# Layers' context attention: rotated keys and first queries computed in the step before

## What is computed

```python
pe_q = rope_freqs(x.shape[1], 32)
pe_k = rope_freqs(ctx.shape[1], 32)
for l in range(4):
    h = rmsnorm(x, sg[l])
    x = attn_block(h, h,   sWq[l], sWk[l], sWv[l], sWo[l], sbo[l], pe_q, pe_q, mask) + x
    h = rmsnorm(x, cg[l])
    x = attn_block(h, ctx, cWq[l], cWk[l], cWv[l], cWo[l], cbo[l], pe_q, pe_k, None) + x
    h = rmsnorm(x, fg[l])
    x = gelu(h @ fW1[l] + fb1[l]) @ fW2[l] + fb2[l] + x

def attn_block(xq, ctx, ...):            # 8 heads of 64
    q = apply_rope(split(xq @ Wq) / 8, pe_q)
    k = apply_rope(split(ctx @ Wk), pe_k)
    a = softmax(where(mask, q @ k.T, -max))
    return (a @ split(ctx @ Wv)) @ Wo + bo
# apply_rope(t): the first 32 of 64 columns become t * cos + rotate_half(t) * sin
```

## Time and profile before

| | us |
|---|---|
| median of 3 runs | 4027.64 (4020.51 to 4027.95) |
| profiled execution | 4024.78 |
| its span, first to last instruction | 4022.6 |
| PE busy | 3721.1 (93%) |
| DVE busy | 2719.0 (68%) |
| ACT busy | 1980.9 (49%) |
| POOL busy | 1015.0 (25%) |
| mean granted PE clock | 0.978 of full speed |

### The profile page before, as it was taken

One profiled execution on the slowest core, in us unless ns is written; L12 is line 12 of the kernel. 1 busy time (PEld: TensorE's weight loads), 2 busy tenths in 40 slices (PEclk: granted clock), 3 DMA queues, 4 the chain that ended last, 5 costly groups with the idle time before them and its releaser, 6 DMA issues.

```text
span 4022.6 us, 70135 instructions
## 1 busy us (share of the span) xinstructions
PE 3721.1 (93%) x22966; PEld 2300.2 (57%) x22966; DVE 2719.0 (68%) x8004; ACT 1980.9 (49%) x5746; POOL 1015.0 (25%) x1109
## 2 busy tenths in 40 slices
PE   6999899999999998999988998999999999989997
PEld 4645446566565664566656444456656556645664
DVE  3787767676777745676456886777777776457663
ACT  1733345555555542576428214456555565317653
POOL 0154433222423301101111562322322232010012
PEclk8999999999999999999989999999999999999998
DMA  2100000001000002010210000000000000100101
GB/s 74 48 18 1 1 24 18 25 1 42 1 18 24 2 26 81 2 70 16 62 57 5 18 1 18 7 18 25 18 25 10 32 1 12 67 30 2 64 16 51
DMA packets 37011, 103.89 MB, mean 26 GB/s; under 512 B 3504, under 2 KB 28592, under 8 KB 33200
## 3 DMA queue, kind: packets, MB, share of 16 engines
q1 hardware_dynamic: 34608, 95.20, 6.6%
q0 software_dynamic: 2048, 4.20, 0.3%
HBM read 90.35 MB, written 9.04 MB: 25 GB/s over the span
## 4 chain that ended last, share of the span: by engine, by line
PE 70%; DVE 15%; ACT 7%; issue 5%; POOL 2%; DMA 0%; DVEq 0%; POOLq 0%; ACTq 0%; SPq 0%
PE ps_O L646 13%; PE ps_P L628 8%; PE ps_S L597 6%; PE ps_OUT L792 4%; PE ps_O L628 4%; PE ps_OUT L597 3%; ACT EX L729 3%; PE ps_P L1374 2%; PE ps_P L1666 2%; PE ps_S L1374 2%; PE ps_P L608 2%; PE ps_P L382 2%; PE ps_T L597 2%; PE ps_O L382 1%; PE ps_OUT L1157 1%
## 5 line engine op out<-in xcount | busy, mean ns | idle before, releaser
L646 PE MATMUL ps_O<-wide,V 128*64 128x256 f32 (+4 forms) x5152 | 595.8, 393 | 1.8 <-ACT wide L674 1.8
L729 ACT ACTIVATE EX<-NB,neg 128x154 f32<-128x154 f32 (+3 forms) x768 | 402.5, 530 | 113.8 <-DVE neg L757 113.8
L692 POOL COPY RX<-recips 128x256 f32<-128x256 f32 (+2 forms) x356 | 156.9, 441 | 1114.0 <-DVE recips L772 1105.4
L597 PE MATMUL ps_S<-KT,QT 64*128 64x154 f32 (+7 forms) x1936 | 373.1, 456 | 60.7 <-POOL QT L1679 25.4
L783 DVE TENSOR_TENSOR QT<-ps_O,RS 128x512 f32<-128x512 f32 x212 | 146.6, 692 | 390.4 <-PE ps_O L646 390.0
L676 DVE COPY wide<-ps_P 128x512 f32<-128x512 f32 (+4 forms) x528 | 340.0, 647 | 73.0 <-PE ps_P L628 69.6
L646 PEld LDWEIGHTS ps_O<-wide,V 128*64 128x64 f32 (+4 forms) x5152 | 266.6, 127 | 194.1 <-issue 110.1
L597 PE MATMUL ps_T<-KT,QT 64*128 64x154 f32 (+5 forms) x968 | 322.6, 436 | 3.5 <-ACT EX L729 3.5
L597 PE MATMUL ps_OUT<-KT,QT 64*128 64x154 f32 (+5 forms) x968 | 325.7, 435 | 0.1
L628 PE MATMUL ps_P<-consts,EX 128*128 128x128 f32 (+1 forms) x1956 | 290.8, 285 | 25.0 <-ACT RS L683 11.7
L729 ACT ACTIVATE QT<-NB,neg 128x512 f32<-128x512 f32 (+2 forms) x512 | 311.8, 618 | 0.0
(11 more groups left out here) (516 smaller groups left out, 8106.4 us busy)
## 6 DMA issues: line engine op xcount, KB each, us to landing
weights<-in_w_dram SPq DMA_DIRECT2D x10, 1664.0 KB, 7.0
weights<-in_w_dram SPq DMA_DIRECT2D x2, 6148.0 KB, 17.2
weights<-in_w5next_dram SPq DMA_DIRECT2D x6, 1664.0 KB, 6.6
weights<-in_w_dram SPq DMA_DIRECT2D x2, 4200.0 KB, 13.7
weights<-in_reltab_dram SPq DMA_DIRECT2D x2, 4096.0 KB, 13.4
weights<-in_w_dram SPq DMA_DIRECT2D x8, 640.0 KB, 3.8
weights<-in_w_dram SPq DMA_DIRECT2D x2, 2050.0 KB, 8.5
weights<-in_w_dram SPq DMA_DIRECT2D x2, 2048.0 KB, 8.1
```

The source lines that it names most:

```text
L597: ins = pe.matmul(S4[k][:, a * N:(a + 1) * N], QT[strip, c, qts[a] * P:(qts[a] + 1) * P], self.keys(c)[strip, 0:N], start=True, stop=True)
L646: ins = pe.matmul(O1[self.slot * j:self.slot * (j + 1), q0 * P:(q0 + self.nq) * P], self.value(c * self.hpc + j, kc), self.probs(rd, j)[:, ...
L692: pool.tensor_copy(RX[:, q0 * P:(q0 + self.nq) * P].rearrange("p (n s) -> p n s", s=self.slot), of.unsqueeze(2).broadcast_to([P, self.nq * ...
L729: ins = act.activation(ex[:, a * N:(a + 1) * N], src, ACT.Exp, bias=neg[:, at:at + 1], scale=-1.0 if self.added else 1.0, accum_out=sums[: ...
```

## The change

The context keys of all four chunks and the queries of chunk 0 are made and rotated in the step before, the host. All keys and the first queries then lie in parts of `picked`, a buffer unused in the layers. Keys are made in two pairs, K0 (chunks 0 and 1) and K1 (chunks 2 and 3), 308 columns wide in one bank each, and Q is the first query product. In the host they are late entries: for lane 1's self attention K0 behind iteration 5, K1 behind 6, Q behind 8; for lane 0's context step K0 behind 1, K1 behind 2, Q behind 4. The context step keeps q1 in its front, and q2 and q3 as late entries. Its scores of round 0 wait for the third add of `ready`, and its PE program waits at the start until Q's bank has been read. In iterations without maxima DVE takes late entries behind the last product with the reciprocals. In POOL's program a context step has only q1's add ahead of the power.

```diff
@@ class Attention @@
             def evacuated(self, eng, r, s):
                 e, n = self.seq[s]
+                if e in self.ahead_done:
+                    eng.wait_ge(*self.ahead_done[e])
+                    return
...
+                for j in self.late.get(self.rounds, ()):
+                    late(pool, j)
...
             def dve(self, dve, r, free=None, beside=None, late=None):
                 for i in range(self.steps):
-                    for j in self.late.get(i - 1, ()):
-                        if j != "X":
-                            late(dve, j)
+                    if i < self.rounds:
+                        self.late_dve(dve, i, late)
...
+                    if i >= self.rounds:
+                        self.late_dve(dve, i, late)
                     if beside:
                         beside(i)
@@ class L1Attention @@
-                self.order = [(m, c) for c in range(4) for m in "kq"]
+                self.order = [("q", c) for c in range(1, 4)] if cross else [(m, c) for c in range(4) for m in "kq"]
+                late = {0: [1], 1: [2], 2: ["X"]} if cross else {1: [4], 2: [5, "X"], 3: [6], 4: [7]}
+                n = L.n
+                self.hosts = n == (0 if cross else 1)
+                if self.hosts:
+                    late = ({0: [1], 1: [2, "K0"], 2: ["X", "K1"], 4: ["Q"]} if cross else
+                            {1: [4], 2: [5, "X"], 3: [6], 4: [7], 5: ["K0"], 6: ["K1"], 8: ["Q"]})
...
+            def ahead_pe(self, pe, j, bank):
+
+                r = self.r
+                self.weights(pe)
+                if j == "Q":
+                    pe.wait_ge(r.xT, 1)
+                    pe.matmul(bank[:, :], self.w("wq")[:, 0:P], self.L.XT[:, :], start=True, stop=True).then_inc(r.part, 1)
+                    return
+                for i in range(2):
+                    c = 2 * int(j[1]) + i
+                    ins = pe.matmul(bank[:, i * CTX:(i + 1) * CTX], self.w("wk")[:, c * P:(c + 1) * P], self.L.CT[:, :],
+                                    start=True, stop=True)
+                ins.then_inc(r.part, 1)
...
+                dve.stream_shuffle(part, bank[:, 0:308], HALVES).then_inc(r.part_used, 1)
+                dve.tensor_tensor(two(to), two(bank[:, 0:308]), every2(K("cos")), ALU.mult).then_inc(r.part_used, 1)
+                dve.wait_ge(r.part_used, 2 * n + 1)
+                dve.tensor_tensor(two(part), two(part), every2(K("sin")), ALU.mult).then_inc(r.gate, 1)
+
+            def ahead_pool(self, pool, j):
...
+                pool.wait_ge(r.part_used, 2 * n + 2)
+                pool.wait_ge(r.gate, n + 1)
+                pool.tensor_tensor(to, to, part, ALU.add).then_inc(r.ready, 1)
...
             def pe(self, pe):
                 r = self.r
                 self.weights(pe)
                 pe.wait_ge(r.xT, 1)
+                if self.cross:
+                    pe.wait_ge(r.part_used, 6)
                 pe_table(pe, r, self.front)
```

More of the change, by code:

```diff
@@ L566, in value, with query @@
                 return V[0:self.kc, c * w + h * self.slot:c * w + (h + 1) * self.slot]
+            def query(self, c):
+                return self.query0 if c == 0 and self.query0 is not None else QT[:, c, :]
             def out_chunk(self, c):
@@ L1618, in __init__ @@
                 self.NK, self.src = NK, src
-                self.order = [(m, c) for c in range(4) for m in "kq"]
-                self.att = Attention(8, 64, NK, added=None if cross else (lambda h, qt: L.maskb[:, :]),
[L1621 to L1624, removed]
+                self.order = [("q", c) for c in range(1, 4)] if cross else [(m, c) for c in range(4) for m in "kq"]
[5 more added lines that the diff above has]
+                            {1: [4], 2: [5, "X"], 3: [6], 4: [7], 5: ["K0"], 6: ["K1"], 8: ["Q"]})
+                store = picked[:, :, :].rearrange("p t d -> p (t d)")
+                self.turnedK = store[:, 616 * n:616 * n + 616]
+                self.partsK = [store[:, 1232 + 308 * i:1540 + 308 * i] for i in range(2)]
+                self.turnedQ = store[:, 1848:2360]
+                keys = (lambda c: self.turnedK[:, c * CTX:(c + 1) * CTX]) if cross else (lambda c: KT[:, c, :])
+                queries = ((lambda c: (self.r.rotated, c) if c else (self.r.ready, 3)) if cross else
+                           (lambda c: (self.r.rotated, 2 * c + 2)))
+                self.att = Attention(8, 64, NK, added=None if cross else (lambda h, qt: L.maskb[:, :]),
+                                     keys=keys, queries=queries, late=late)
+                if cross:
+                    self.att.query0 = self.turnedQ
+                self.fronts = 1 if cross else 4
+                ropes = [([self.product(j)], P, self.size(j), "D", "rope", self.dest(j), self.turning(j))
+                         for j in range(self.fronts)]
                 values = [([(src[:, c * kc:(c + 1) * kc], w("wv"))], kc, SEQ, "A", "copy",
@@ L1682, in pool @@
                 self.fresh(pool)
-                self.rotate(pool, 0)
-                self.rotate(pool, 1)
+                for j in range(1 if self.cross else 2):
+                    self.rotate(pool, j)
                 self.prev.pool_tail(pool)
@@ L1687, in pool @@
                     self.nxt.pool_head(pool)
-                self.rotate(pool, 2)
-                self.rotate(pool, 3)
+                for j in range(2, self.fronts):
+                    self.rotate(pool, j)
                 if self.prev.tail_parts > 1:
@@ L1700, in pe @@
                 self.att.x_done = self.nxt.r.xT
+                if self.hosts:
+                    nr = self.nxt.r
+                    self.att.ahead_done = {"K0": (nr.part_used, 2), "K1": (nr.part_used, 4), "Q": (nr.part_used, 6)}
                 self.att.pe(pe, r, ready=[(r.evac_act, self.front.a), (r.evac_dve, self.front.d)], wo=self.w("wo"),
```

45 lines of the change are left out of this document (40 added, 5 removed).

## The result

The changed kernel takes **4041.2 us** (median of 6 runs, 4039.56 to 4051.62); the kernel before, on the same chip, 4024.07 (6 runs, 4018.28 to 4038.10). The ratio is 1.0046, 95% interval 1.0032 to 1.0059: slower by 0.46%, where I forecast 4024.6 and a range up to 4037. The profiled executions took 4042.21 and 4024.78. In the experiments, "against" is the kernel before, timed beside the run on the same chip.

A forecast was written before the change was run, and what follows sets the result against it. The head was taken as bound by DVE's time to the first maximum plus an unchanged chain. 1.90 - 0.15 - 2.13 = -0.38 per layer of a pair, times 8 = -3.0 us: 4024.6, range 4009 to 4037.

The forecast's parts named there:

- From the first maximum to 699.58 everything shifts by the same 2.13: Context step's head: the first maximum starts 2.13 us earlier and the whole chain behind it moves equally.
- 1 to 2 us for exponentials at round 1: Expected sign in the head: PE waits this long ahead of round 1's scores, instead of waiting for POOL.
- three signs of being wrong: Scaling takes 0.2, round 1's transposes wait over 1 us, or the hosts hide the moved products.
- Self attention: Lane 1, as host: two pairs of key products (4 x 0.26) and one query product (0.86), +1.90 us.
- the new wait at the step's start: PE at the context step's start waits for the query rope until about T + 0.1, over 1.5 us slack behind.
- Lane 0's context step without a fall: Head 2.13 shorter, plus 0.60 bank wait, 0.52 for K1's products and 0.86 for Q: -0.15 us.
- K0's wait for the bank: Lane 0's context step: round 1's transposes wait for K0's bank, 0.57, taken as 0.60 us.
- Lane 1's without a fall: Lane 1's context step hosts nothing and gets shorter by 2.13 us.
- the rule: DVE operation with two SBUF inputs and POOL operation reading SBUF exclude one another: K0's sine product waits 0.6, sum unchanged.
- my faster rival: Scaling in the head not blocked by POOL's add: 0.95 more per head, 15.2 us in all, 4009; chance 0.20.
- PE is waiting for POOL by name only: Head: POOL is named releaser of 0.96 and 0.63 us waits, but DVE's time to the first maximum sets its length.
- The slower one: POOL's add also holds K0's cosine product: bank wait 1.58 instead of 0.60, up to +9.0 us, 4037; chance 0.20.

The follow-up runs named there:

- e6: Changed kernel with two filler products (512 and 384 columns, results overwritten) behind q2 in every context step; 4029.17 against 4026.11, ratio 1.0001.
- e15: Kernel before with one 384-column filler product behind q2, in the 0.63 us idle ahead of round 1's scores; one execution, 4031.39.
- e8: Changed kernel with only the first queries made in the host, keys as in the kernel before; one execution, 4028.48.
- e2: Changed kernel with both key pairs behind iteration 2 of lane 0's context step; 4050.44 against 4039.90, ratio 1.0028.
- e5: Kernel before with squares and scaling behind round 0's maxima, POOL's power behind k1's and q1's adds; 4021.20 against 4026.11, ratio 0.9980.
- e14: Changed kernel with squares and scaling behind round 0's maxima and both key pairs behind iteration 2; 4019.05 against 4040.99, ratio 0.9952.
- e10: Kernel before with one filler product (0.86 us) in the 0.96 us gap ahead of round 0's scores; 4045.87 against 4043.97, ratio 1.0006.
- e13: Changed kernel with the two filler products (512 and 384 columns) in lane 0's context step only; one execution, 4067.43.
- e1: Changed kernel with one 512-column filler product (0.86 us) behind q2 in every context step; 4045.94 against 4039.90, ratio 1.0013.
- e3: Changed kernel with the squares and their scaling moved behind round 0's maxima in context steps; 4015.17 against 4039.90, ratio 0.9941.
- e11: Repeat of e3: changed kernel with squares and scaling behind round 0's maxima in context steps; ratio 0.9924 to the kernel before.
- e7: Changed kernel with only the keys made in the host, first queries in the context step's own front; one execution, 4039.35.
- e9: Changed kernel with only first queries made in the host, squares behind round 0's maxima, power behind q1's add; 4030.13 against 4043.97, ratio 0.9959.

## Why the prediction was wrong

**The step that failed** is the sentence "From the first maximum to 699.58 everything shifts by the same 2.13". The first maximum did shift, round 1's scores with it (T' + 6.68, where they had started at T + 8.94), and without falls the rest followed: in e6 the transposes of the reciprocals start at 701.77 - 686.76 = 15.01 behind the step's start, where the prediction gives 17.23 - 2.13 = 15.10. In the changed kernel it is 15.95, because the clock falls on the way. PE ends q2 at T' + 5.12, 3.19 earlier in the step than before, but round 1's scores come only 2.26 earlier; so PE idles 1.57 in one place, where it had 0.96, 0.53 and 0.63 in three. I wrote that wait down myself ("1 to 2 us for exponentials at round 1") and priced it at nothing. None of the three signs of being wrong that I named came: the scaling took 1.11, the transposes' wait was 0.72, and the hosts hid nothing.

*Size.* Falls cost 144.27 - 141.81 = 2.46 in the changed kernel and 141.84 - 141.24 = 0.60 in the kernel before: 1.86 more for a layer and pair, **14.9 us of the 19.4** (the profiled executions of e6 and e15 stand for the kernels without falls). The rest of the miss is mis-sized terms:

- *Self attention*: +1.90 forecast, +2.64 measured. A pair of key products took 0.72, twice, not 0.52; the query product 0.97, not 0.86; and the last output projection 2.18 (682.29 to 684.47) where before it took 1.89, as PE meets the new wait at the step's start: 0.20 + 0.20 + 0.11 + 0.29 = 0.80, about the 0.74 that were missing. That wait I had called free by its slack of 1.5 us; it delays the front by 0.29 by these rows. e8, whose self attention is 1.20 longer with the query product alone, leaves 0.23 for it.
- *Lane 0's context step without a fall*: 38.31 against 38.03 forecast (38.18 - 0.15). K1 and Q took 0.68 and 0.96 instead of 0.52 and 0.86. K0's wait for the bank was 0.47 of idle time in e6's trace, 0.63 from start to start as the forecast's 0.60 was counted. As a cost that term isn't borne out: e2's one step without a fall, which has no such wait but one of 0.69 for ACT, is only 0.07 shorter.
- *Lane 1's without a fall*: 35.92 against 36.05. Right.

Without falls in either kernel the change costs 141.81 - 141.24 = 0.57 for a layer and pair, 4.5 us, where I had -3.0: within 0.2% both. That part of the forecast, "within", would have held, by the step lengths.

**K0's sine product** was held for 0.6, as the rule gave it: 1.05 in the row at 702.25, beside POOL's add of 701.70 to 702.97, where the same operation takes 0.47 alone. In the Trainium skill, SBUF — State Buffer, section "SBUF: two separate sides", such a pair excludes one another for the whole instruction; the 1.22 in e5 agrees (0.31 alone; POOL's add ends at 690.48, the product at 690.66). **The scaling** stayed blocked, as forecast; my faster rival had nothing for it.

**"PE is waiting for POOL by name only"** was half right. With fewer operations on DVE ahead of the maxima (the change) the first maximum came earlier by what DVE lost. But e5 shows POOL's adds close behind as a bound of the old head: 1.57 less on DVE brought the first maximum 0.65 earlier and the step's end 0.25.

**The rivals.** The slower one (K0's bank, 4037) named a wrong mechanism: K0's cosine product was not held (0.46 at 701.87, beside the same POOL add), and e14 shows the wait to be nearly slack. I gave no chance to the clock, although the trace of before had a fall in 4 of 16 heads; a range built on one head at full clock left it out. That its 4037 lies near the measured 4041.2 is luck.

**What stays open**: why the same head falls in one step and not in the next (4 of 16 before and 7 in e10, 6 of 8 in lane 1 after, 8 of 8 in e13), why lane 0 keeps all its falls in e1 where lane 1, with the same gap of 0.71, keeps one of 8, and how the length of the gap and the work around it combine. The experiments show which gap it is, and that filling it whole or taking it away ends the falls.

## What to carry to other kernels

Before multiplying one instance, list all instances with their lengths and granted clocks: here the steps of the same instructions that were longer were those with a lower clock, and they showed what one more wait can trigger. Where work is taken from a full PE and the chain behind it doesn't get shorter, the time becomes idle time, and that can cost more than it saved: 1.57 us of it led to 1.6 us more in lane 0's step. A filler product into such a gap tells whether it is so, if it fills the gap: e1's half filling left all of lane 0's falls. The cure is to shorten the chain that the gap waits for, which here turned a 0.46% loss into a gain of 0.6 to 0.8% (e3, e11).

## What the hardware showed beyond this

- The granted clock falls behind gaps of well under 2 us in a stretch that is otherwise dense: with one of 1.57 (after, 14 of 16 steps), of 1.00 (e7, 9), of 0.71 (e1, 8 of 8 steps of lane 0), of 0.62 or 0.63 (before, e5, e8, e9 and e10, 3 to 7 of 16); never in e3, e6, e11, e14 and e15, where that gap is closed. In the Trainium skill, TensorE: Matmul & The Clock Gate, section "A second HAM failure mode: psum-queue depth-cycling", small idle times between groups of matmuls bring such an oscillation in another kernel, a bf16 one; these fp32 traces agree: 14 of 16 heads at 1.57, none of 16 in e6.
- The gap's place counts: 0.96 us ahead of round 0's scores, filled or not, decided nothing (filled in e10: 7 falls of 16; open in e15: none), 0.63 ahead of round 1's did (e15). Behind the latter the score products have a wait of 0.22 between them, behind the former none; whether that is the reason, no run shows.
- A POOL add holds a small DVE operation too: the scaling, 128x4, takes 1.11 beside an add and 0.17 behind it (e3). The add is longer as well, 1.39 beside the scaling and 1.27 in e3.
